# Letting the last relation of a graph layer start its sums from nothing, and adding them to u by accumulating DMAs

## The reference

```
h   = relu(layernorm(x))                                   # 1250 x 1024, float32
u   = h @ root + bias
for r in range(8):                                         # relational mean over incoming edges
    mask = (edge_type == r)
    sums = segment_sum(h[src] * mask, dst, 1250)
    cnt  = segment_sum(mask, dst, 1250)
    u    = u + (sums / max(cnt, 1)) @ weight[r]
z   = concatenate([u, h], axis=1) @ w_gate + b_gate        # w_gate: 2048 x 1024
out = x + tanh(u) * z + h * (1 - z)
```

## Time and profile before

| | us |
|---|---|
| median of three runs | 1355.16 |
| the profiled execution's own time | 1356.57 |
| its span, first to last instruction | 1354.8 |
| TensorE busy | 1270.8 |
| VectorE busy | 950.1 |
| GpSimd busy | 775.5 |
| ScalarE busy | 425.4 |
| mean granted TensorE clock | 0.988 |

### The profile page before, as it was taken

The page is one execution under the profiler, slowest core; times in us unless marked ns, Lnnn a source line. Parts: engine busy times, 40 slices in busy tenths (PEclk is TensorE's granted clock), DMA queues, the critical chain, the costliest instruction groups (busy, mean ns, idle before and its releaser), DMA issues.

```text
span 1354.8 us, 19982 instructions
## 1 busy us (share of the span) xinstructions
PE 1270.8 (94%) x6167; PEld 641.1 (47%) x6167; DVE 950.1 (70%) x1296; ACT 425.4 (31%) x526; POOL 775.5 (57%) x857
## 2 busy tenths in 40 slices
PE   3899999999999999999999999999999889988998
PEld 1445444444444444544454445544545444434565
DVE  6779798476556767776677567656685657787886
ACT  4472213234324423221322133222311111575200
POOL 6322068787878866686677666777684734331000
PEclk9999999999999999999999999999999989998999
DMA  6371125252134258776776988698788986687976
GB/s 229 128 272 60 43 62 162 55 170 56 38 102 123 64 179 274 217 218 228 249 220 197 325 262 284 221 293 277 246 264 263 347 280 186 189 268 219 243 228 212
DMA packets 111323, 269.44 MB, mean 199 GB/s; under 512 B 21526, under 2 KB 22029, under 8 KB 111236
## 3 DMA queue, kind: packets, MB, share of 16 engines
q1 hardware_dynamic: 75204, 175.64, 38.9%
q0 software_dynamic: 36032, 92.64, 24.0%
HBM read 199.47 MB, written 87.30 MB: 212 GB/s over the span
## 4 chain that ended last, share of the span: by engine, by line
PE 58%; DVE 13%; DMA 10%; issue 9%; ACT 4%; POOL 4%; POOLq 1%; SPq 0%; DVEq 0%; ACTq 0%
PE ps L1372 49%; PE ps L1334 9%; DMA early<-y_rows,pair 6%; POOL onehot L663 2%; DVE W L1005 2%; DMA early<-u_rows 2%; DVE hT L1053 1%; POOL early L655 1%; DMA W<-in_L_gnn_weight_dram 1%; ACT W L769 1%; DMA u_rows<-early 1%; DVE wspread L983 1%; ACT hT L847 1%; ACT peek_out L736 1%; DVE early L1216 1%
## 5 line engine op out<-in xcount | busy, mean ns | idle before, releaser
L1372 PE MATMUL ps<-W,hT 128*128 128x512 f16 (+2 forms) x4740 | 1064.9, 381 | 12.5 <-DVE W L1005 8.2
L1372 PEld LDWEIGHTS ps<-W,hT 128*128 128x128 f16 (+2 forms) x4740 | 475.5, 103 | 527.2 <-issue 21.3
L626 POOL DMA_INDIRECT table_rows<-edges,early x160 | 248.2, 1551 | 114.6 <-issue 114.6
L655 POOL DMA_INDIRECT early<-y_rows,pair x192 | 228.7, 1191 | 86.5 <-PE ps L1337 46.1
L1334 PE MATMUL ps<-early,onehot 128*125 x768 | 198.4, 385 | 34.1 <-DVE early L1216 13.3
L663 POOL TENSOR_SCALAR onehot<-iota_d,pair 128x125 f16<-128x125 f16 x180 | 151.6, 842 | 90.1 <-DMA early<-y_rows,pair 84.5
L1005 DVE SCALAR_TENSOR_TENSOR W<-W,wsc 128x2048 f16<-128x2048 f32 x62 | 148.1, 2390 | 16.9 <-ACT W L769 16.9
L819 ACT ACTIVATE yhl<-early 128x512 f16<-128x512 f32 x100 | 62.8, 628 | 302.9 <-DVE early L1127 178.2
L769 ACT ACTIVATE W<-W,wsc 128x2048 f16<-128x2048 f32 x62 | 122.7, 1991 | 101.8 <-DVE W L1021 49.3
L1334 PEld LDWEIGHTS ps<-early,onehot 128*125 x768 | 102.4, 137 | 107.5 <-issue 59.3
L736 ACT ACTIVATE peek_out<-W 128x1024 bf16<-128x1024 f32 x80 | 84.2, 1053 | 139.1 <-DMA W<-in_L_gnn_weight_dram 64.0
(11 more groups left out here) (192 smaller groups left out, 849.8 us busy)
## 6 DMA issues: line engine op xcount, KB each, us to landing
y_rows<-yhl SPq DMA_DIRECT2D x144, 256.0 KB
W<-in_L_gnn_weight_dram SPq DMA_DIRECT2D x30, 1024.0 KB, 8.3
u_rows<-early SPq DMA_DIRECT2D x50, 448.0 KB
early<-u_rows SPq DMA_DIRECT2D x30, 448.0 KB
W<-in_L_gnn_w_gate_dram SPq DMA_DIRECT2D x8, 1024.0 KB, 8.2
early<-in_x_dram SPq DMA_DIRECT2D x9, 512.0 KB, 5.5
hs_rows<-early SPq DMA_DIRECT2D x9, 512.0 KB, 4.1
root_rows<-yhl SPq DMA_DIRECT2D x18, 256.0 KB
```

What stands on the lines that cost most here:

```text
L626: pool.indirect_dma_start(out=table_rows, out_offset=bass.IndirectOffsetOnAxis(ap=at_i[:, c:c + 1], axis=0), in_=packed[0:EP, c:c + 1], in ...
L655: pool.indirect_dma_start(out=G[:, b, :], out_offset=None, in_=y_rows[i], in_offset=bass.IndirectOffsetOnAxis(ap=idx[:, b, :], axis=0), bo ...
L1372: last = nc.tensor.matmul(ps[0:rows, n % 4, :], hT[:, m, v_h, k, n0:n0 + rows], Wh[MAT[w][c]][:, v_w, k, :], start=(first and v_h + v_w == ...
```

## The change

1. The last sweep starts each tile of u from nothing: `add_group` writes sum times scale with one tensor_scalar and waits for no load. Its tiles are stored to new rows `last_rows`. Its ten loads of u are not issued.
2. In the closing `load_sum` loads the u of the sweep before the last. An accumulating DMA adds root's rows to it in `cu` (`add_root`), and a second one adds the last sweep's rows (`add_last`). GpSimd's tensor_tensor and the two buffers for root's rows are gone; ScalarE waits for the second accumulation. `add_last` of tile j stands behind `add_root` of tile j + 1.
3. The last sweep's groups are spread over 24 tenths of a unit step instead of 21: they end behind unit 270 instead of 267.
4. The scan's factors get a small tile of their own (125 x 800), written once at GpSimd's start, and all 16 scans read it.
5. For `gate_u` the matmul `weight_max` and VectorE's `weight_scale` both stand at n = 300.

```
-              + [209 + g * 39 // 20 for g in range(20)] + [249 + g * 21 // 10 for g in range(10)])
+              + [209 + g * 39 // 20 for g in range(20)] + [249 + g * 24 // 10 for g in range(10)])
...
+        FAC = NG // SN * EC
+        factors = qflat[0:EP, 11 * EC:11 * EC + FAC // 2].bitcast(BF16)
...
 (store_u, SyncE)
+                    to = last_rows if sweep == NS - 1 else u_rows
+                    sp.dma_start(to[n0:n0 + rows, :], ub[p0:p0 + rows, k % 3, :]).then_inc(s[f"u_stored{k % 3}"], 16)
...
-                        if NJ <= k + 2 < len(STEPS):
+                        if NJ <= k + 2 < len(STEPS) - NJ:
                             load_u(k + 2)
...
 (GpSimd's start, ahead of table_i's memset)
+            pool.memset(factors, 1.0).then_inc(s["factors_ready"], 1)
+            pool.wait_ge(s["factors_ready"], 1)
+            pool.memset(factors.rearrange("p (g c) -> p g c", c=EC)[:, :, 0:1], 0.0).then_inc(s["factors_ready"], 1)
...
             for i in range(NJ):
                 split_low(i)
-                if i < 2:
-                    scan_factors(2 * i)
-                    scan_factors(2 * i + 1)
...
             def load_sum(j):
-                k = len(STEPS) - NJ + j
+                k = len(STEPS) - 2 * NJ + j
...
+            def add_root(j):
                 for n0, p0, rows in halves(*DTL[j]):
+                    pool.dma_start(cu[j % NCU][p0:p0 + rows, :], root_rows[n0:n0 + rows, :],
+                                   accum_op=ALU.add).then_inc(s[f"cu_rooted{j % NCU}"], 16)
...
+            def add_last(j):
+                k = len(STEPS) - NJ + j
+                pool.wait_ge(s[f"u_stored{k % 3}"], 32 * u_stores(k))
+                pool.wait_ge(s[f"cu_rooted{j % NCU}"], 32 * (j // NCU + 1))
+                for n0, p0, rows in halves(*DTL[j]):
+                    pool.dma_start(cu[j % NCU][p0:p0 + rows, :], last_rows[n0:n0 + rows, :],
+                                   accum_op=ALU.add).then_inc(s[f"cu_summed{j % NCU}"], 16)
+
             for j in range(NJ):
-                u = cu[j % NCU][0:DT, :]
-                pool.wait_ge(s[f"cu_loaded{j % NCU}"], 32 * (j // NCU + 1))
-                pool.wait_ge(s[f"root_loaded{j % 2}"], 32 * (j // 2 + 1))
-                pool.tensor_tensor(u, u, root_in[j % 2][0:DT, :], ALU.add).then_inc(s["u_rooted"], 1)
-                if j + 2 < NJ:
-                    pool.wait_ge(s["u_rooted"], j + 1)
-                    load_root(j + 2)
+                if j == 0:
+                    pool.wait_ge(s["cu_loaded0"], 32)
+                    add_root(0)
+                if j + 1 < NJ:
+                    pool.wait_ge(s[f"cu_loaded{(j + 1) % NCU}"], 32 * ((j + 1) // NCU + 1))
+                    add_root(j + 1)
+                add_last(j)
                 if j >= 2 and j + 2 < NJ:
                     pool.wait_ge(s[f"cu_stored{(j - 2) % NCU}"], 32 * ((j - 2) // NCU + 1))
                     load_sum(j + 2)
...
 (u_size, ScalarE)
-                act.wait_ge(s["u_rooted"], j + 1)
+                act.wait_ge(s[f"cu_summed{j % NCU}"], 32 * (j // NCU + 1))
...
 (scan_part, VectorE)
-                nc.vector.tensor_tensor_scan(out=part, data0=part, data1=hot[:, g0 * EC:g1 * EC], initial=0.0,
+                nc.vector.tensor_tensor_scan(out=part, data0=factors, data1=hot[:, g0 * EC:g1 * EC], initial=0.0,
...
 (add_group, VectorE)
-                    if sweep:
+                    if 0 < sweep < NS - 1:
                         dve.wait_ge(s[f"u_loaded{b}"], 32 * u_loads(k))
...
-                if r == 0:
+                if sweep == NS - 1:
+                    nc.vector.tensor_scalar(ub[0:DT, b, :], sums, inv[0:DT, 1:2], None, ALU.mult).then_inc(s["u_added"], 1)
+                elif r == 0:
...
 (VectorE's loop, then TensorE's)
-                if n - 3 in TOPS:
+                if TOPS.get(n - 3, W_GU) < W_GU:
                     weight_scale(TOPS[n - 3])
+                if TOPS.get(n - 4) == W_GU:
+                    weight_scale(W_GU)
...
-                if n - 2 in TOPS:
+                if TOPS.get(n - 2, W_GU) < W_GU:
                     weight_max(TOPS[n - 2])
+                if TOPS.get(n - 4) == W_GU:
+                    weight_max(W_GU)
```

More of the change, by code:

```diff
@@ L177, in gated_rgcn_preln @@
     u_rows = nc.dram_tensor("u_rows", [N, D], F32).ap()
+    last_rows = nc.dram_tensor("last_rows", [N, D], F32).ap()
     root_rows = nc.dram_tensor("root_rows", [N, D], F32).ap()
@@ L310, in gated_rgcn_preln @@
         uhl = [G[:, b, :] for b in (0, 1)]
-        root_in = [G[:, b, :].bitcast(F32) for b in (2, 3)]
         cu = [ub[:, (NS * NJ - 3 + b) % 3, :] for b in range(3)] + [G[:, 4, :].bitcast(F32)]
@@ L326, in gated_rgcn_preln @@
         at_i = table_i[0:EP, 0:EC]
+        FAC = NG // SN * EC
+        factors = qflat[0:EP, 11 * EC:11 * EC + FAC // 2].bitcast(BF16)
+        assert 11 * EC + FAC // 2 <= HT * HC and NG % SN == 0
         eflat = edges[:, :, :].rearrange("p t b -> p (t b)")
@@ L356, in gated_rgcn_preln @@
             *(f"u_loaded{b}" for b in range(3)), *(f"u_stored{b}" for b in range(3)),
-            "u_added", *(f"cu_loaded{b}" for b in range(4)), *(f"cu_stored{b}" for b in range(4)), "root_loaded0", "root_loaded1", "u_rooted", "u_summed", "us_ready", "u_hi", "u_lo", "tanh_ready", "uT_a", "uT_b", "uT_a_out", "uT_b_out",
+            "u_added", *(f"cu_loaded{b}" for b in range(4)), *(f"cu_stored{b}" for b in range(4)), *(f"cu_rooted{b}" for b in range(4)), *(f"cu_summed{b}" for b in range(4)), "u_summed", "us_ready", "u_hi", "u_lo", "tanh_ready", "uT_a", "uT_b", "uT_a_out", "uT_b_out",
             *(f"z_loaded{b}" for b in range(NZ)), "res_ready", *(f"out_stored{b}" for b in range(NZ)))}
@@ L434, in store_u @@
                 for n0, p0, rows in halves(*DTL[j]):
-                    sp.dma_start(u_rows[n0:n0 + rows, :], ub[p0:p0 + rows, k % 3, :]).then_inc(s[f"u_stored{k % 3}"], 16)
+                    to = last_rows if sweep == NS - 1 else u_rows
+                    sp.dma_start(to[n0:n0 + rows, :], ub[p0:p0 + rows, k % 3, :]).then_inc(s[f"u_stored{k % 3}"], 16)
             def store_closed(j):
@@ L698, in load_sum @@
                     pool.dma_start(cu[j % NCU][p0:p0 + rows, :], u_rows[n0:n0 + rows, :]).then_inc(s[f"cu_loaded{j % NCU}"], 16)
-            def load_root(j):
+            def add_root(j):
                 for n0, p0, rows in halves(*DTL[j]):
-                    pool.dma_start(root_in[j % 2][p0:p0 + rows, :], root_rows[n0:n0 + rows, :]).then_inc(s[f"root_loaded{j % 2}"], 16)
+                    pool.dma_start(cu[j % NCU][p0:p0 + rows, :], root_rows[n0:n0 + rows, :],
+                                   accum_op=ALU.add).then_inc(s[f"cu_rooted{j % NCU}"], 16)
             pool.wait_ge(s["u_added"], NG)
@@ L710, in _ @@
                 pool.wait_ge(s[f"y_stored{b}"], 16 * NJ * 2 * (W_ROOT + 1) // 4)
-            for j in range(2):
-                load_root(j)
-            for j in range(NJ):
-                u = cu[j % NCU][0:DT, :]
-                pool.wait_ge(s[f"cu_loaded{j % NCU}"], 32 * (j // NCU + 1))
-                pool.wait_ge(s[f"root_loaded{j % 2}"], 32 * (j // 2 + 1))
-                pool.tensor_tensor(u, u, root_in[j % 2][0:DT, :], ALU.add).then_inc(s["u_rooted"], 1)
-                if j + 2 < NJ:
-                    pool.wait_ge(s["u_rooted"], j + 1)
-                    load_root(j + 2)
+            def add_last(j):
[5 more added lines that the diff above has]
+                                   accum_op=ALU.add).then_inc(s[f"cu_summed{j % NCU}"], 16)
+            for j in range(NJ):
+                if j == 0:
[5 more added lines that the diff above has]
+                add_last(j)
                 if j >= 2 and j + 2 < NJ:
@@ L1055, in scan_part @@
                                              saturate=False))
-                dve.wait_ge(s["factors_ready"], 2 * (b * SQ // SN + 1))
+                dve.wait_ge(s["factors_ready"], 2)
                 part = scan[:, g0 * EC:g1 * EC]
-                nc.vector.tensor_tensor_scan(out=part, data0=part, data1=hot[:, g0 * EC:g1 * EC], initial=0.0,
+                nc.vector.tensor_tensor_scan(out=part, data0=factors, data1=hot[:, g0 * EC:g1 * EC], initial=0.0,
                                              op0=ALU.mult, op1=ALU.add).then_inc(s["scan_ready"], 1)
```

## The result

The kernel after takes 1365.45 us (median of 13 runs, 1361.24 to 1371.93) against 1356.84 for the kernel before on the same chip (13 runs): a ratio of 1.0066, 95% interval 1.0049 to 1.0083. It is slower by 9 us where 16 us of gain were forecast. Its profiled execution took 1366.21 us with a span of 1364.5, against 1356.57 and 1354.8.

The account below looks back on a forecast made before the run. TensorE, busy 1270.8 of 1354.8 us, was taken as the bound, so only its waits and half-clock time could go. Start -6.2, last sweep -10.9 and closing +1 gave -16.1: forecast 1339 us, range 1332 to 1349.

Parts of the forecast that it names:

- Start, -6.2: Kernel start: two long VectorE `wspread` shrink once the factors are small, winning 4.0 and 2.2 us; bounds 4.0 to 8.8.
- Last sweep, -10.9: Last sweep: 9.5 us won by dropping the loads of u, 1.4 by wider spacing; bounds 7 to 13.9.
- Closing, +1: Closing: +2.7 for tile 7, +2.3 for tiles 4 and 5, -4 returned; bounds -6 to +8 us.
- Tile 0: Closing's first tile: load and two accumulations take 19.7 us, leaving it 3 us late, which costs TensorE nothing at first.
- From tile 3 on: Closing: each tile waits for the tanh store three tiles back, then 13.1 us to its sum, against 3.4 before.
- 3 to 6: Closing: the lateness in us forecast for tiles 4 and 5, whose sums wait for a store.
- Tiles 3 and 6: Closing: forecast, with tiles 8 and 9, not to come out late.
- The -4 returned: Closing from 1193 us on: VectorE instructions no longer stretched beside GpSimd's additions give back some 4 of 11 us.
- tile 7's 2.7: Closing: tile 7's sum comes 2.7 us late and, through `weight_scale`'s new place, adds that to TensorE's wait before unit 305.
- Rival 1: Closing: accumulations take 12.8 us each, ScalarE waits at `cu_summed`, closing +23.5, total 1361.5 us; chance 6 in 100.
- three signs that were to show me wrong: Accumulations landing in over 10 us, last sweep idle 6 us or more, or the start's 6.2 not found at 500 us.
- The rule weighed in the prediction: GpSimd DMA: about 2.0 us fixed plus bytes at 436 GB/s; with it no closing tile late by more than 2 us.

Follow-up runs that it names:

- parts 3 and 4 alone: The kernel before with only the small factors tile and the 24-tenths group spacing, last sweep still loading u: 1347.9 us, ratio 0.9889.
- part 4 alone: The kernel before with only the scan's factors moved to a small tile of their own: 1353.0 us, ratio 0.9957.
- one accumulation: The kernel after with root's rows added by GpSimd's tensor_tensor, last rows by accumulating DMA, five buffers: 1353.1 us; with part 5 also undone, 1351.0.

## Why the prediction was wrong

- **Start, -6.2.** Right: 6.0, and 0.43% as an edit by itself.
- **Last sweep, -10.9.** 13.0 came, 12.6 of it in the sweep itself. In the order of the prediction both terms are near: the loads that go were given 9.5 and brought 9.9 (97.0 to 87.1), the spacing behind them was given 1.4 and brought 2.7 (87.1 to 84.4). What the prediction never asked is what the spacing is worth by itself: 9.8 (97.1 to 87.3), since three more units between the groups hide a late load nearly as well as a late evacuation. With it in place part 1 is worth 2.9 us, and part 1 alone brought the closing's second addition.
- **Closing, +1.** This is the step that failed: +27.6 was measured. What it had wrong is the landing of an accumulation (5.5 us) and of the load beside it (4.5), and the loop that these stand in, which it did not price. Split by the experiments at the same landmarks, from before's 109.8: 2.4 up to 112.2, 5.0 for part 5 (117.2), 4.2 for three plain loads in series in place of two and GpSimd's addition (121.4), 16.0 for the accumulating itself (137.4). The ratios say the same: 0.9862, 0.9911, 0.9946, 1.0066. The 2.4 stand in parts 3 and 4 alone as well (112.1) and not in part 4 alone (110.1): the spacing ends the sweep three units nearer to the closing. The pieces come from one profile each and hold in this order; taken out of after, part 5 gives nothing.
  - *Tile 0* was right, and not by luck. It was given 19.7 us from the first issue of a load, which came at 1116.60; `u_size(0)` started at 1136.52, 19.9 later.
  - *From tile 3 on* the sum was to come 13.1 us behind a store. Tile 3's came 1171.31 - 1151.11 = 20.2 behind it: the load took 8.5 to land and be noticed where 1.04 + 4.5 were given, root's accumulation 1.1, the last one 10.6 where 1.04 + 5.5 were given. The 5.5 was the wrong size (medians 7.0 and 8.6), and so was the plain load's 4.5, taken from a closing with two transfers a tile (5.8 with three plain ones, 7.3 with the accumulations).
  - *The loop.* The forecast asked only what one store delays. It never closed the circle load, `add_root(j + 1)`, `add_last(j)`, load, which takes 12.7 to 16.3 us a tile against 9 with no wait for a store in it. That is why the lateness grows tile by tile instead of staying at 3 to 6. Tiles 3 and 6, which were to come in time, made ScalarE wait 9.98 and 4.61 us too.
  - *The -4 returned.* The stretched additions are gone as said (the line's longest is 0.76 us, 2.87 before), but VectorE waits for sums, and no return is to be seen. No run isolates it.
- **Part 5.** The direction was right (the wait before unit 305 rose from 3.71 to 7.96), the price, tile 7's 2.7, too small: 5.0 when the sums come in time (117.2 against 112.2), and 4.0 with one accumulation (125.0 against 121.1).
- **Rival 1** named the right place, `cu_summed`, and nearly the time (1361.5), but by another mechanism, and there the nearness is luck: the median accumulation is 7.0 to 8.6 us, not 12.8, and the circle runs through the load in four turns of five, not through the store. 6 in 100 was too little for an operation of which no row existed.
- Of the three signs that were to show me wrong, none came clearly: accumulations land in under 10 us at the median, though nine of the forty do not (4.9 to 13.0), the sweep has 2.2 us of idleness, and at 491 us 5.4 of the start's gain is there (6.2 in part 4 alone). The signs tested each part; none watched the pace of the loop they form.

## What to carry to other kernels

Before giving a late transfer a new place, try giving its consumer a few units more: one number won 9.8 us of the last sweep here, where a second set of rows, forty accumulating DMAs and a new order won 9.9 and lost more behind it. When an operation has no row in the trace, price the loop it stands in and not its latency alone, with everything in the same queue slowed by it. And when an edit's cost is hidden by a wait, measure it again with that wait gone.

## What the runs showed of the hardware

- An accumulating DMA from device memory into a tile on the chip (float32, 448 and 52 KB) costs the DMA engines more than a plain one. GpSimd's queue took 56.2% of the engines' time for 15.09 MB, two thirds of it accumulated, against 40.7% for 15.36 MB all plain: 2.65% a MB plain, so by estimate 4.3% a MB accumulated, 1.6 times as much. By windows it is a share of 0.93 at 237 GB/s, and 1.04 at 221 back to back, against 0.80 at 258 with plain loads. The plain load's median beside it goes from 5.8 to 7.3 us. Where the accumulations ran back to back, a 1 MB weight quadrant took up to 24.4 us to land, against 7.20 in the chain of before; how much of that is the accumulating and how much the crowding is open.
- Its issue costs GpSimd more as well: 1.68 us for the first pair in a turn, 1.04 for a plain pair.
- The rule weighed in the prediction (the Trainium skill, DMA: Bandwidth & Descriptors, Anatomy of one DMA — SWDGE (gpsimd) path) gives, as an estimate, 3.05 us for 448 KB; no landing of these loads was that short (3.6 at the least before, 3.5 with plain loads, 3.8 in after), so in this traffic it is a lower bound only.
